# Two attentions of a four-stage kernel: the first one's statistics spread over its ticks, the second one's block-diagonal keys written by on-chip transfers alone

## The reference

```python
# L0: x, kv as (8, 128 channels, 256 positions); 16 heads of 8 channels
q, k, v = Wq @ x + bq, Wk @ kv + bk, Wv @ kv + bv
attn = softmax(where(kv_mask, (q * 8**-0.5) @ k.T, -inf))          # 256 x 256 per head
mean = attn @ v
std = sqrt(relu(attn @ (v * v) - mean * mean))
x = x * mask
mu = x.sum(-1) / n_valid
var = (x * x).sum(-1) / n_valid - mu * mu
xn = (x - mu) / sqrt(relu(var) + 1e-5) * mask
out = (xn * std + mean) * mask

# L1: 4 batches; x: 256 context rows, latents: 32 rows of the result above
q = latents @ q_w + q_b                                             # 16 heads of 16
kmat, v = heads(concat([x, latents]) @ kv_w + kv_b)
attn = softmax(where(full_mask, q @ kmat.T / 16, -inf))
y = rmsnorm((attn @ v) @ out_w + out_b + latents) * postnorm_w
out = gelu(y @ mlp_w1 + mlp_b1) @ mlp_w2 + mlp_b2 + latents
```

## Time and profile before

| what | value |
| --- | --- |
| median of 3 runs | 1185.3 us (1183.77 to 1189.86) |
| the profiled execution | 1191.5 us |
| its span, first to last instruction | 1189.6 us |
| mean granted clock of TensorE | 0.966 |
| TensorE busy | 1061.8 us (89%) |
| VectorE, ScalarE, GpSimd busy | 729.0, 719.9, 318.0 us |

### The profile page before, as it was taken

One profiled execution on the slowest core, in us unless ns is written; L12 is line 12 of the kernel. 1 busy time (PEld: TensorE's weight loads), 2 busy tenths in 40 slices (PEclk: granted clock), 3 DMA queues, 4 the chain that ended last, 5 costly groups with the idle time before them and its releaser, 6 DMA issues.

```text
span 1189.6 us, 23809 instructions
## 1 busy us (share of the span) xinstructions
PE 1061.8 (89%) x8128; PEld 934.1 (79%) x8128; DVE 729.0 (61%) x1747; ACT 719.9 (61%) x2082; POOL 318.0 (27%) x433
## 2 busy tenths in 40 slices
PE   4899897789978999999998989999999789688798
PEld 3677676577758989999997869999998779667588
DVE  5677685677786646555555645555555575567773
ACT  2577775678884456656565556666565543588851
POOL 5234333766540012211111103111111120243410
PEclk9799999899999999999999999999999979799999
DMA  5211111011101021111101011110011110100100
GB/s 158 64 28 46 40 28 51 17 24 26 45 22 50 18 90 45 45 45 46 45 32 62 20 45 45 45 42 20 30 45 44 46 36 1 49 16 19 47 10 27
DMA packets 29851, 48.07 MB, mean 40 GB/s; under 512 B 6627, under 2 KB 20389, under 8 KB 29734
## 3 DMA queue, kind: packets, MB, share of 16 engines
q1 hardware_dynamic: 29734, 46.56, 12.5%
HBM read 36.54 MB, written 1.05 MB: 32 GB/s over the span
## 4 chain that ended last, share of the span: by engine, by line
PE 66%; DVE 12%; ACT 11%; issue 7%; POOL 2%; DMA 1%; SPq 1%; DVEq 0%; ACTq 0%; POOLq 0%
PE ps L753 14%; PE ps L755 14%; PE ps L754 14%; PE ps L983 4%; PE ps L959 4%; ACT pt L1237 3%; PE ps L1113 3%; PE ps L968 2%; PE ps L887 2%; PE ps L1100 1%; DVE nm L1766 1%; PE ps L1091 1%; PE ps L910 1%; DVE nmax L1569 1%; POOL pt L1817 1%
## 5 line engine op out<-in xcount | busy, mean ns | idle before, releaser
L1817 POOL TENSOR_TENSOR pt<-pt,prec 128x256 f32<-128x256 f32 (+1 forms) x224 | 180.9, 808 | 629.5 <-DVE prec L1638 500.1
L1292 ACT ACTIVATE pt<-ps,nmax 128x129 f32<-128x129 f32 x256 | 92.3, 367 | 100.6 <-DVE nmax L1630 99.8
L753 PE MATMUL ps<-rs 128*128 128x256 f32 x480 | 145.0, 302 | 3.4 <-DVE rs L1652 2.9
L1433 DVE TENSOR_TENSOR rs<-wraw,rs 128x256 fp32r<-128x256 f32 (+2 forms) x116 | 69.3, 600 | 124.0 <-ACT rs L1168 123.6
L755 PE MATMUL ps<-rs 128*128 128x256 f32 x480 | 138.0, 287 | 0.0
L754 PE MATMUL ps<-rs 128*128 128x256 f32 x480 | 138.0, 287 | 0.0
L1237 ACT ACTIVATE pt<-ps,nmax 128x256 f32<-128x256 f32 (+1 forms) x256 | 105.3, 425 | 44.6 <-DVE nmax L1569 33.2
L753 PE MATMUL ps<-ht,rs 128*128 128x256 f32 (+1 forms) x304 | 108.4, 357 | 9.5 <-DVE X L1591 3.1
L754 PE MATMUL ps<-ht,rs 128*128 128x256 f32 (+1 forms) x304 | 101.7, 335 | 0.0
L755 PE MATMUL ps<-ht,rs 128*128 128x256 f32 (+1 forms) x304 | 101.6, 334 | 0.0
L753 PEld LDWEIGHTS ps<-rs 128*128 128x128 f32 x480 | 93.9, 196 | 6.5 <-DVE rs L1652 5.0
(11 more groups left out here) (201 smaller groups left out, 2989.6 us busy)
## 6 DMA issues: line engine op xcount, KB each, us to landing
wraw<-in_packs SPq DMA_DIRECT2D x52, 512.0 KB, 3.7
rs<-rs SPq DMA_DIRECT2D x224, 32.0 KB, 1.9
bvr<-in_l2rows SPq DMA_DIRECT2D x16, 256.0 KB, 4.6
rs<-rs SPq DMA_DIRECT2D x96, 16.0 KB
row<-in_rows SPq DMA_DIRECT2D x2, 640.0 KB, 6.5
XH<-in_packs SPq DMA_DIRECT2D x2, 512.0 KB, 3.8
out<-X SPq DMA_DIRECT2D x4, 256.0 KB, 2.1
X<-in_x SPq DMA_DIRECT2D x3, 256.0 KB, 2.9
```

Source lines behind the costliest of these rows:

```text
L753: nc.tensor.matmul(dst, w[0], m[1], start=start, stop=False)
L1292: last = nc.scalar.activation(prob[:, g % 3, k * D:k * D + P + 1], ps[:, S_BANK + g % 2, k * D:k * D + P + 1], ACT.Exp, bias=nmax[:, g % 4 ...
L1433: last = nc.vector.tensor_tensor(dst[1], src, f32(dst[0]), ALU.subtract)
L1817: nc.gpsimd.tensor_tensor(pr, pr, prec[:, u % 4, 0:nh].unsqueeze(2).broadcast_to([P, nh, keys]), ALU.mult)\
```

## The change

1. **Statistics of the first attention.** `xs` moves from ticks 2 + 2b to 10b (10 to 70), with the closing chain behind that of sequence 7; the mask of sequences 1 to 7 goes behind the statistics of sequence 0, the second attention's mask to tick 3 (`m2`). The square root `sq` goes to tick 84, its reciprocal on VectorE to tick 86 (`rs`), and `xn` to ticks 87 to 90 and 104, 112, 120, 128. `xn` now reads X in place of a masked copy, `OUT` waits for the sequence's statistics in place of `xn`, and `mul` moves to 91 and 93 with a wait for `xn`.
2. **Start.** Before the first selection product TensorE computes 8 products that nobody reads (`warm`), and 9 more before the first score. Two of the first step's four block transfers are issued by ScalarE.
3. **Keys of the second attention.** `pk` is gone for L1: no selection product, no mask product, no copies. `key_rows` writes both halves: 12 transfers per step and 4 mask rows on the first two steps of an iteration. TensorE waits for all of them before the first unit of the step. L3 keeps its form.

```diff
-    "L1": dict(iters=4, keys=256, units=2, key_tiles=2, stack_a=2, stack_d=1),
+    "L1": dict(iters=4, keys=256, units=2, key_tiles=2, stack_a=1, stack_d=0),
...
         if b:
-            put(2 + 2 * b, "xs", b)
-        put(16 * b + 24, "xn", b)
+            put(10 * b, "xs", b)
+        put(87 + b if b < 4 else 72 + 8 * b, "xn", b)
...
-    put(20, "sq", 0)
+    put(3, "m2", 0)
+    put(84, "sq", 0)
+    put(86, "rs", 0)
...
-    prep = {"L1": [(0, "pq", 0), (1, "pk", 0)], "L3": [(0, "pq", 0), (0, "pk", 0)]}[ph]
+    prep = {"L1": [(0, "pq", 0)], "L3": [(0, "pq", 0), (0, "pk", 0)]}[ph]
...
-                for j in range(4):
-                    r = slice(32 * j, 32 * j + 32)
-                    sp.dma_start(kbd[s % L0_BLOCKS][r, j, :].bitcast(F32), qk[r, s % L0_STACKS, D:2 * D].bitcast(F32))\
-                      .then_inc(kb_in[s % 2], 16)
+                for j in range(2 if s == 0 else 4):
+                    sp.dma_start(*key_block(s, j)).then_inc(kb_in[s % 2], 16)
...
+                groups = (0, 1) if ph == "L1" else (1,)
+                blocks = ks[ph][s % 2][:, 0:4 * n].rearrange("p (g m h n) -> p g h m n", g=2, m=2, h=2).bitcast(F32)
                 if m < 2:
+                    for g in groups:
+                        for j in range(2):
+                            sp.dma_start(blocks[64 * j + 48:64 * j + 49, g, j, :, 0:P],
+                                         mb13[0:1, 2 * it * P:(2 * it + 2) * P].rearrange("p (m n) -> p m n", m=2).bitcast(F32))\
+                              .then_inc(ks_in[s % 2], 16)
+                sp.wait_ge(a["dense"], dense_at(ph, it, "dk", m // 2 if ph == "L1" else 0))
+                for g in groups:
                     for j in range(2):
...
+                        r = 32 * ((2 * m + g) % 4) + 16 * j
+                        for part in range(3):
+                            sp.dma_start(blocks[64 * j + 16 * part:64 * j + 16 * part + 16, g, j, :, :],
...
                     if ph == "L1":
-                        if r == 1:
+                        if r == 0:
                             rows_moved(pe, ph, s)
...
+            def warm(n):
+
+                for _ in range(n):
+                    nc.tensor.matmul(ps[:, L0_O, 0:D], w0[:, 0, :], X[:, 0, :], start=True, stop=True)
...
                     if s == 0:
+                        warm(8)
                         pe.wait_ge(Z["mask"], 1)
...
+                    if i == 0:
+                        warm(9)
                     if j == 0:
                         pe.wait_ge(kb_in[s % 2], 64 * (s // 2 + 1))
...
                     nc.scalar.activation(qk[:, i % L0_STACKS, :], bank, ACT.Identity, bias=C("ones0")).then_inc(Z["st"], 1)
+                    if i == 0:
+                        act.wait_ge(Z["st"], 1)
+                        act.wait_ge(Z["zero"], 1)
+                        for j in (2, 3):
+                            act.dma_start(*key_block(0, j)).then_inc(kb_in[0], 16)
```

More of the change, by code:

```diff
@@ L133, in first_order @@
     put(121, "w", "L1sel1")
-    for k, (dev, mul, res, lat) in enumerate([(84, 87, 92, 119), (None, 91, 97, 123), (150, 152, 155, 160), (None, 154, 158, 164)]):
+    for k, (dev, mul, res, lat) in enumerate([(84, 91, 95, 119), (None, 93, 99, 123), (150, 152, 155, 160), (None, 154, 158, 164)]):
         if dev:
@@ L147, in first_order @@
         (units[-1] if units else head).append(e)
-    for tick, e in zip((130, 131, 133, 145, 147, 134, 135), head, strict=True):
+    for tick, e in zip((130, 131, 133, 145, 147, 134), head, strict=True):
         put(tick, *e, st="L1")
@@ L591, in rows_moved, with key_block @@
         def rows_moved(eng, ph, s):
-            before = 0 if ph == "L1" else 6 * 2 * STEPS + 2 * 4
-            eng.wait_ge(ks_in[s % 2], 16 * (before + 6 * (s // 2 + 1) + 2 * (s // STEPS + 1)))
+            steps, quarters = s // 2 + 1, s // STEPS + 1
+            moved = 12 * steps + 4 * quarters if ph == "L1" else (12 * 2 * STEPS + 4 * 4) + 6 * steps + 2 * quarters
+            eng.wait_ge(ks_in[s % 2], 16 * moved)
+        def key_block(s, j):
+            r = slice(32 * j, 32 * j + 32)
+            return kbd[s % L0_BLOCKS][r, j, :].bitcast(F32), qk[r, s % L0_STACKS, D:2 * D].bitcast(F32)
         def taken(eng, name):
@@ L657, in key_rows @@
                     sp.wait_ge(a["sm"], 2 * c["units"] * (s - 1))
-                blocks = to.rearrange("p (m h n) -> p h m n", m=2, h=2).bitcast(F32)
+                groups = (0, 1) if ph == "L1" else (1,)
+                blocks = ks[ph][s % 2][:, 0:4 * n].rearrange("p (g m h n) -> p g h m n", g=2, m=2, h=2).bitcast(F32)
                 if m < 2:
-                    for j in range(2):
[L661 to L667, removed]
-                        sp.dma_start(blocks[64 * j + 16 * part:64 * j + 16 * part + 16, j, :, :],
-                                     dense_keys(ph, part // 2, it, m)[r:r + 16, :].rearrange("p (m n) -> p m n", m=2).bitcast(F32))\
-                          .then_inc(ks_in[s % 2], 16)
+                    for g in groups:
[5 more added lines that the diff above has]
+                for g in groups:
+                    for j in range(2):
+                        r = 32 * ((2 * m + g) % 4) + 16 * j
+                        for part in range(3):
+                            sp.dma_start(blocks[64 * j + 16 * part:64 * j + 16 * part + 16, g, j, :, :],
+                                         dense_keys(ph, part // 2, it, m)[r:r + 16, :].rearrange("p (m n) -> p m n", m=2).bitcast(F32))\
+                              .then_inc(ks_in[s % 2], 16)
             def pack(n):
@@ L860, in att @@
                         pe.wait_ge(a["stA"], c["stack_a"] * (s + 1))
-                        pe.wait_ge(a["stD"], c["stack_d"] * (s + 1))
+                        if ph == "L3":
+                            pe.wait_ge(a["stD"], c["stack_d"] * (s + 1))
                     n = len(SCORE_BANKS[ph])
@@ L1041, in l0 @@
                     return
[L1042 removed]
+                if e in ("w", "m2", "sq", "rs", "dev", "mul", "res", "zk", "zv", "dl", "vq", "vr"):
                     return
@@ L1354, in l0 @@
                 elif e == "sq":
-                    act.wait_ge(l0stat, 1)
+                    act.wait_ge(l0stat, B + 1)
                     act.wait_ge(eps_ok, 1)
@@ L1500, in x_stats @@
                         link(last)
+                    else:
+                        last.then_inc(l0stat, 1)
                     return
@@ L1718, in l0 @@
                 if e == "xs":
-                    if i == 1:
+                    x_stats(i)
+                    if i == 0:
                         key_mask(slice(D, B * D))
-                    if i == 2:
-                        second_mask()
-                    x_stats(i)
                     if i == B - 1:
                         x_stats(B)
-                elif e == "sq":
+                elif e == "m2":
+                    second_mask()
+                elif e == "rs":
                     dve.wait_ge(l0sq, 1)
@@ L1904, in l0 @@
                     pool.wait_ge(l0dev, i // 2 + 1)
+                    pool.wait_ge(xn_done, 2 * i + 2)
                     nc.gpsimd.tensor_tensor(X[:, two, :], X[:, two, :], ms[:, 1, two, :], ALU.mult).then_inc(l0mul, 1)
```

8 lines of the change are left out of this document (3 added, 5 removed).

## The result

The changed kernel takes 1201.0 us (median of 4 runs, 1199.9 to 1202.9) against 1187.6 us of the kernel before on the same chip (median of 4 runs, 1183.8 to 1190.5): a ratio of 1.0107, 95% interval 1.0083 to 1.0131. The ratios of this document are formed over all runs and differ by up to 0.001 from the quotient of the medians. The change is slower, and its time lies 1 us above the top of the forecast's range. The profiled execution took 1200.7 us, its span is 1199.0.

A forecast was written before the change was run, and what follows sets the result against it. VectorE's queue was taken to bound the first attention's start, TensorE its settled part, SyncE's issue queue the changed second attention. First attention -9 and second +12.5 gave +3.5 us, carried to the median 1189 us; range 1177 to 1200.

The forecast's parts named there:

- Idle time goes with it: Second attention: removing key products also removes TensorE idle, so a settled step shortens 0.9 us, 0.53 of it work.
- an issue queue that doesn't fit into the round: Second attention: SyncE needs about 38 us of transfer issues in a round of 33.4 us, making key groups late.
- First attention, what goes: First attention's start: statistics leaving VectorE's queue, idle and half clock going with them, gain 11.5 us by tick 32.
- the clock from the first score on: First attention: a sign of being right, TensorE's clock at 1.00 from the first score on.
- First attention, what comes: First attention: returning statistics and closing chain cost 2.0 us, fillers 0.5 us; block transfers and GpSimd work 0.
- the fillers' sum: First attention's start: eight fillers from 6.1 us end between 10.2 and 12.9 us; fillers in all +0.5 us.
- Second attention, what goes: Second attention: without key products and copies a settled step shortens 0.9 us; the first round gains 4 us.
- Second attention, what comes: Second attention: late key groups cost 16.5 us, the start 4.5 us before shortening is deducted, the clock 1.8 us.
- The sum: Whole kernel: first attention -9 us, second attention +12.5 us, third stage 0, together +3.5 us.
- The base: Whole kernel: profiled span 1189.6 us (run 1191.5), taken as 0.5% over a median of 1185.3 us.
- Rival 2: Second attention: issues at 0.68 us, half clock after each late group, rounds of 40 us; 1195 us, chance 0.25.
- Rival 1: Second attention: transfers stay hidden, wholly or nearly, rounds from the second on below 36.5 us; 1177 us, chance 0.20.
- Rival 3: First attention: block transfers or fillers hold the start, score 17 at 34 us; 1194 us, chance 0.08.

The follow-up runs named there:

- e2: The kernel before with only the change's new keys of the second attention: 1207.1 us, ratio 1.0167.
- e10: The changed kernel without the second attention's mask rows and key low-half transfers, both also left out of the computation (8 issues a step): 1182.5 us, ratio 0.9957.
- e1: The changed kernel with the second attention's keys as before, so the first attention's part alone: 1184.9 us, ratio 0.9978.
- e7: The first attention's part alone (second attention's keys as before), without the 17 filler products at the start: 1179.1 us, ratio 0.9920.
- e12: The same code as e1, measured once more: ratio 0.9972.
- e4: The changed kernel with 6 to 12 filler products on TensorE before the key waits of six second-attention steps: 1202.3 us, ratio 1.0118.
- e3: The changed kernel without the second attention's mask-row transfers, its mask left out of the computation (12 issues a step): 1184.3 us, ratio 0.9966.
- e8: The changed kernel with selection products kept for half the keys in each round's first two steps, and the first attention's late pieces moved: 1181.6 us, ratio 0.9932.
- e11: e8 without the 17 filler products at the start: 1179.8 us, ratio 0.9934.

## Why the prediction was wrong, point by point

1189 us were forecast and 1201.0 came. Of the 12 us, 5.8 are terms of the sum, read from the profiles: 3.0 from the second attention, 1.9 from the first, 0.9 from the rest. The step that failed is "Idle time goes with it": a step was to shorten by 0.9 us and shortened by 0.4. The other 6.2 us are the base. The main mechanism, an issue queue that doesn't fit into the round, was right.

- **First attention, what goes: right.** 11.5 us by tick 32 were forecast, 12.9 came; the 17th score at 32.1 (31.6), the 33rd at 51.1 (near 52), the clock at 1.00 from 27 us on. One sign failed, the clock from the first score on: 22 to 27 us read 0.66. And some of the 12.9 is the profile of before: e2, whose first attention is the old one, reaches the 33rd score at 62.4 us, not 63.9.
- **First attention, what comes: too small.** 2.5 us were put back, TensorE's stops say 5. Stops of 0.6 us and more from score 33 to 160 us (170 before) add up to 7.6 us before and 12.6 after. New are 1.58 at 90.5 us instead of 0.77, 1.71 at 105.3, 1.09 at 142.5 and 1.05 at 149.9. The forecast spread the five statistics evenly and took 40% of them; but the last statistic and the closing chain of six stand together at tick 70, and the results `res` were moved from ticks 92 and 97 to 95 and 99, which the sum never priced. The stop at 105.3 (timelines of VectorE and TensorE, changed kernel):

```profile
102.81 0.41 DVE L1517 CUSTOM_DVE_ANT_0 fs<-X,mt 128x256 f32<-128x256 f32 x1
103.16 0.08 DVE L1517 DVE_READ_ACCUMULATOR2_ANT sd<- 128x1 f32 x1
103.27 1.38 DVE L1519 CUSTOM_DVE_ANT_0 fs<-fs 128x256 f32<-128x256 f32 x1
...
105.80 0.17 DVE L1531 TENSOR_SCALAR sd<-sd 128x8 f32<-128x8 f32 x1
105.91 0.42 DVE L1797 TENSOR_TENSOR rs<-ps,rs 128x256 fp32r<-128x256 f32 x1
106.25 1.87 DVE L1790 TENSOR_REDUCE nm<-ps 128x2 f32<-128x512 f32 x3
...
106.98 0.50 PE L1108 MATMUL ps<-rs 128*128 128x512 f32 x1 [1.71 <-DVE nm L1790]
```

  From 102.9 to 106.2 VectorE works on no row maximum, and TensorE, three banks ahead, runs dry. Nearly 1 us of this is the statistic's second pass, which takes 1.38 us in place of 0.42 (see the last section). In all the second attention starts 7.1 us earlier, not 9. (A slip in the fillers' sum, 10.2 for 6.1 + 3.4, moves nothing: the first selection product came at 11.4 us, 0.9 later than before, and the first score at 16.5 as before.)
- **Second attention, what goes: the mis-sized term.** The forecast let a step shorten by 0.9 us, 10.3 us in all with the first round; e10, where nothing waits for the queue, shows 3.2 us in the first round, 1.5 in the second and third, 0.4 a step, and 0.8 in the fourth: 7.0. Against e1, e7 and e12, which have the keys as before, it is 5.0 to 6.3. The 0.53 us of matmul work a step was right: busy time fell by 1.95 us a round, 0.49 a step. The wrong step is "Idle time goes with it": the stops beside the key products were of the first round; in the settled ones the 2.65 us of idle ended with other things and stayed, 3.1 in e10.
- **Second attention, what comes: right in sum, in part by luck.** Between e10 and the change lie 22.5 us (2.7, 5.4, 7.4, 7.0 by rounds). The forecast had 4.5 at the start, 16.5 for late groups and 1.8 for the clock: 22.8. Within it errors cancel: the start costs 2.7 and not 4.5, the later rounds 19.8 and not 18.3. Both late groups of a round count, 5.1 us of waits in round 3 (3.34 and 1.72), and there TensorE is busy 2.4 us longer with the same products (31.15 against 28.71). The latter is no cause of its own: e4 took most of the half clock away and won next to nothing, so those 2.4 us fill time that TensorE would wait. The issues were as read from the earlier trace rows, 0.64 us from one to the next; with one long issue of 1.52 us among them the 16 took 11.2 us (271.33 to 282.53) and not 10.5, and step 8's first score came 12.7 us after its group had started, not 11.8.
- **The sum.** -7.1 + 15.5 + 0.9 is +9.3 by the profiles, where +3.5 was forecast. The 0.9 behind the second attention, put at 0, says little: that part takes 836.5 to 842.6 us in the fourteen profiles, though its code is the same.
- **The base.** The forecast took the profiled 1191.5 us for 0.5% above a median of 1185.3. More runs put the median at 1187.4 to 1189.0, while the profile of the change lies at its median. Between the 1189 forecast and 1201 about 6 us are terms of the sum and the other 6 are this: 2.3 us of median, and 4 us by which the one profile of before was long. By e2, whose last score of the first attention comes at 185.6 us and not 187.2, about 1.5 of the 4 may lie there; where the rest lies stays open. How far one profile can be off is shown by e1 and e12, one and the same code, which start the second attention at 196.5 and 200.2 us; in the medians the first half of the change is worth 2.5 to 4 us, not the 9.2 between the profiles of before and e1 at that point.
- **Rival 2 was the nearest**: rounds of 40 us, slower, 1195. Its mechanism is shown in e3 and e10, but not its half about the clock: e4 took away 17 us of half clock and won 1. Rival 1, hidden transfers, is out for the change and describes e10, where the queue has room. The rule of the Trainium skill behind it (DMA: Bandwidth & Descriptors, Rules for kernel authors), to issue early and wait late, does hold in e10, at 8 issues a step; at 16 "early" does not exist. A neighbouring line of the same section says to coalesce many small transfers, since below 64 KB one pays mostly overhead: here a 1 KB mask row held SyncE for 0.57 us, a 32 KB key transfer for 0.59 us (medians of the change), and e3 agrees. Rival 3 fell: the start did speed up.

## What to carry to other kernels

Count the issues of a queue against the period in which they must be done (here 56 times 0.68 us in 33), group by group from the moment the buffer comes free; a share of busy engines doesn't show it, the queue's timeline and the wait ahead of the consumer do. Whether a second engine's queue could have taken half of the issues was not tried. Of work removed beside such a limit count only the busy time of the bounding engine, and idle time only where a row shows that the removed work ended it, in the same stretch. Before small gains are summed from one profile, ask how two profiles of the same code differ: here 3.7 us at the border on which the forecast counted 9.

## What the runs showed of the hardware

The second pass of a statistic (L1519, before L1497) takes 0.42 us, but 1.38 in one place of the change and 1.37 in one of before (at 24.80 us), and in e12 the first pass takes 1.54. In each of the three a long two-operand instruction of GpSimd runs at the same time, and VectorE's ends about 0.3 us after it (GpSimd, changed kernel; it ends at 104.36, VectorE's at 104.65):

```profile
102.80 1.56 POOL L1897 TENSOR_TENSOR rs<-fs,rs 128x512 fp32r<-128x512 f32 x1
```

GpSimd's casts and small products beside the other statistics cost nothing, and one single-input pass of 0.95 us cost 0.07. The Trainium skill (SBUF — State Buffer, Terms, the entry on the shared port pair) says that VectorE and GpSimd take a pair of ports by an exclusive lock for a full instruction, the loser standing still; the three long passes agree. So does GpSimd's side: its instruction takes 1.56 us here, beside VectorE's first pass of 0.41, and 1.29 in e8, beside none. Of the fourteen profiles twelve have one such long pass; e8 and e11, which moved the last statistic away from GpSimd's instruction, have none above 0.49 us. The long pass counts as busy time of VectorE. No run removed GpSimd's instruction itself.

Of SyncE's issues for the second attention's keys 5 of 112 last over a microsecond before, 7 of 224 after, 7 of 192 in e3 and 3 of 128 in e10. In the two full queues they mostly come 11 to 19 us apart; what causes them is open.
